# A graph kernel's attention weights: the second multiply of each group reads its exponentials in SBUF and not from a PSUM copy

## What is computed

```python
w_m = (efeat @ W_msg + b_msg).reshape(E, 16, 16)
w_a = (efeat @ W_attn + b_attn).reshape(E, 16, 16)
h_src = feat[src][:, :, None]
e1, e2 = w_m * h_src, w_a * h_src
ex = exp(e2 - segment_max(e2, dst)[dst])
attn = ex / segment_sum(ex, dst)[dst]
ft = segment_sum(e1 * attn, dst).sum(axis=1)
x = layernorm(x + ft)
x = layernorm(x + segment_mean(edge_attr, dst))
```

## Time and profile before

| what | us |
|---|---|
| median of 3 executions (2994.75 to 3017.14) | 3010.83 |
| span of the profiled execution, first to last instruction | 2950.2 |
| TensorE matmuls busy | 2137.9 (72%) |
| DVE (VectorE) busy | 1862.0 (63%) |
| POOL (GpSimd) busy | 1687.5 (57%) |
| ACT (ScalarE) busy | 1256.9 (43%) |
| mean granted TensorE clock | 0.861 |

### The profile page before, as it was taken

The page is one execution under the profiler, slowest core; times in us unless marked ns, Lnnn a source line. Parts: engine busy times, 40 slices in busy tenths (PEclk is TensorE's granted clock), DMA queues, the critical chain, the costliest instruction groups (busy, mean ns, idle before and its releaser), DMA issues. The chain is left out here.

```text
span 2950.2 us, 21765 instructions
## 1 busy us (share of the span) xinstructions
PE 2137.9 (72%) x6682; PEld 952.6 (32%) x6682; DVE 1862.0 (63%) x2907; ACT 1256.9 (43%) x1228; POOL 1687.5 (57%) x1845
## 2 busy tenths in 40 slices
PE   2347676676877777877787658877787767887777
PEld 1213233232333333333333223333333323333333
DVE  6246465566666666666676547766667656786776
ACT  3223443434444443454454325444444444554444
POOL 6556355665655565555565465655656565655633
PEclk8658888897988888989888889988989888988988
DMA  6000000000000000000000000000000001001000
GB/s 229 16 10 11 8 12 10 10 10 9 10 9 9 14 10 9 10 14 10 10 13 9 9 10 13 10 12 9 10 12 9 12 9 28 12 8 16 8 2 3
DMA packets 60073, 47.60 MB, mean 16 GB/s; under 512 B 28366, under 2 KB 55439, under 8 KB 59436
## 3 DMA queue, kind: packets, MB, share of 16 engines
q0 software_dynamic: 57632, 29.73, 8.0%
q1 hardware_dynamic: 2316, 16.38, 1.5%
HBM read 44.00 MB, written 1.90 MB: 16 GB/s over the span
## 5 line engine op out<-in xcount | busy, mean ns | idle before, releaser
L652 POOL DMA_INDIRECT AR<-in_xt,AR x1607 | 1538.8, 958 | 974.1 <-DVE AR L1472 491.3
L1128 PE MATMUL PX<-AR,CS 128*128 128x512 f32 x3246 | 1663.7, 642 | 37.8 <-issue 23.9
L1472 DVE CUSTOM_DVE_ANT_1 AR<-PW,AR 128x1024 f32<-128x1024 f32 x815 | 979.6, 1221 | 896.8 <-remote 651.2
L1108 PE MATMUL PW<-WS,LT 100*128 100x512 bf16 x1630 | 549.1, 423 | 683.9 <-DVE AR L1472 511.8
L1128 PEld LDWEIGHTS PX<-AR,CS 128*128 128x128 f32 x3246 | 664.9, 206 | 652.1 <-issue 532.4
L888 ACT ACTIVATE LT<-PTB 100x1024 bf16<-100x1024 bf16 (+1 forms) x221 | 211.2, 956 | 1005.7 <-remote 601.0
L1485 DVE TENSOR_TENSOR AR<-AR,PX 128x1024 f32<-128x1024 f32 (+1 forms) x442 | 501.0, 1134 | 121.3 <-ACT PX L944 76.0
L1108 PEld LDWEIGHTS PW<-WS,LT 100*128 100x128 bf16 x1630 | 141.5, 103 | 1113.7 <-DVE AR L1472 543.2
L946 ACT ACTIVATE AR<-AR 128x2048 f32<-128x2048 f32 (+1 forms) x221 | 412.9, 1869 | 7.2
L950 ACT ACTIVATE PX<-AR 128x1024 f32<-128x1024 f32 (+1 forms) x221 | 212.4, 961 | 412.3 <-DVE AR L1485 294.8
L944 ACT ACTIVATE PX<-AR 128x1024 f32<-128x1024 f32 (+1 forms) x221 | 231.0, 1045 | 39.4 <-DVE AR L1485 30.1
(11 more groups left out here) (192 smaller groups left out, 517.7 us busy)
## 6 DMA issues: line engine op xcount, KB each, us to landing
AR<-in_xt,AR POOLq DMA_INDIRECT x1607
AR<-in_eat SPq DMA_DIRECT2D x3, 3128.0 KB
AR<-in_eat SPq DMA_DIRECT2D x1, 3120.0 KB
y_d<-AR SPq DMA_DIRECT2D x1, 784.0 KB
AR<-y_d SPq DMA_DIRECT2D x1, 784.0 KB
AR<-in_es,E0I POOLq DMA_INDIRECT x48
y_d<-AR POOLq DMA_INDIRECT x36
CS<-in_cst SPq DMA_DIRECT2D x1, 442.0 KB, 5.3
```

Of the source, the lines that this page charges most:

```text
L652: g.indirect_dma_start(feat(h, j - j0, j - j0 + 1), None, xt, bass.IndirectOffsetOnAxis(ap=node, axis=0)).then_inc(hg_sem(h), 16)
L1108: i = pe.matmul(PAIRS[s % 2][:, j, :], LT[:, g % 3, lo:lo + 128], WS[:, :], start=True, stop=True)
L1128: i = pe.matmul(PDR, IDN, x, start=(a == 0 and j == 0), stop=(g == LAST[k] and j == n - 1))
L1472: v.tensor_tensor_reduce(em(g, j, j + 2).rearrange("p (x c) -> p x c", c=32), w, hb, 1.0, LOW, ALU.mult, ALU.max, accum_out=MXC[:, k % 2, ...
```

## The change

ScalarE's third pass (L950) and the two waits in front of it are gone, so ScalarE makes two passes. `gm(g, 1)` waits for the second pass (`a_exp`) and reads the exponentials where they lie, in `EMR`, beside the messages: its two inputs and its output are all in SBUF, in runs of 16 floats with a stride of 32. `gm(g, 0)` is as before. `EXP` is now free as soon as `gm(g, 0)` is done, so the next group's first pass waits for `v_gm` at 2c - 1 and not at 2c. The semaphore `a_x` counts once per group and not twice.

```diff
                         if c >= 1:
-                            a.wait_ge(S["v_gm"], 2 * c)
+                            a.wait_ge(S["v_gm"], 2 * c - 1)
                         a.activation(half(w), x[:, 0:w, :], ACT.Exp, bias=shift).then_inc(S["a_x"], 1)
-                        a.wait_ge(S["a_x"], 2 * c + 1)
+                        a.wait_ge(S["a_x"], c + 1)
                         a.activation(x, x, ACT.Exp, bias=shift).then_inc(S["a_exp"], 1)
-                    if c is not None:
-                        a.wait_ge(S["a_exp"], c + 1)
-                        a.wait_ge(S["v_gm"], 2 * c + 1)
-                        a.activation(half(w), x[:, w:2 * w, :], ACT.Copy).then_inc(S["a_x"], 1)
...
                 def gm(g, h):
                     w = 8 * GRP[g][2]
-                    v.wait_ge(S["a_x"], 2 * g + 1 + h)
-                    y = em(g).rearrange("p (x a o) -> p x a o", a=2, o=16)[:, w * h:w * h + w, 1, :]
-                    v.tensor_tensor(y, y, EXP[:, 0:16 * w].rearrange("p (x o) -> p x o", o=16), ALU.mult).then_inc(S["v_gm"], 1)
+                    y = em(g).rearrange("p (x a o) -> p x a o", a=2, o=16)[:, w * h:w * h + w, :, :]
+                    if h == 0:
+                        v.wait_ge(S["a_x"], g + 1)
+                        powers = EXP[:, 0:16 * w].rearrange("p (x o) -> p x o", o=16)
+                    else:
+                        v.wait_ge(S["a_exp"], g + 1)
+                        powers = y[:, :, 0, :]
+                    v.tensor_tensor(y[:, :, 1, :], y[:, :, 1, :], powers, ALU.mult).then_inc(S["v_gm"], 1)
```

## The result

| kernel | median, us | lowest to highest | profiled span | time of that execution |
|---|---|---|---|---|
| before | 3012.53 (4 executions) | 2994.75 to 3017.14 | 2950.2 | not recorded with its profile |
| after | 2929.38 (4 executions) | 2920.58 to 2939.08 | 2929.3 | 2931.18 |

The ratio is 0.9752, with a 95% interval of 0.9708 to 0.9797. The prediction was wrong, in its sign too.

A forecast was written before the change was run, and what follows sets the result against it. The prediction saw waits as the bound, with DVE held at its feature multiply until shortly after POOL's gather bursts pause. Its terms, -12 + 0 + 0 + 2 + 30 + 2 = +22 us on 3010.8, gave 3033 us, range 2985 to 3085.

The forecast's parts named there:

- the coupling: DVE's remote waits in front of L1472: a longer burst of POOL's gathers was said to hold DVE longer.
- the +30 us: What slower gathers on POOL cost in the end: +30 us, somewhat under half of bounds 0 and 71.
- the lengthening: POOL's gathers L652, held by multiplies with two SBUF inputs: mean from 958 to about 1,000 ns, 71 us in all.
- full price: Rival: every burst passes its lengthened gathers on to DVE, +63 us, 3074 us; chance 0.28.
- absorbed: Rival: POOL's longer gathers come wholly out of its own waits, -8 us, 3003 us; chance 0.14.
- relief: Rival: L888 and L944 are late because of L950, so other waits go too, -67 us, 2944 us; chance 0.12.
- the factor 0.77: Share of the time POOL is in a burst of gathers, applied to 92 us to give 71.
- The multiply: DVE's second multiply with two SBUF inputs instead of one: 1,226 against 1,217 ns, 2 us over 221.
- DVE held by POOL: DVE's multiplies slowed by gathers starting beside them: taken as 2 us, with 18 us as the bound.
- a rival at +60: Rival: a DVE multiply that finds a gather under way stands for its rest, 60 us more, 3093 us; chance 0.05.
- ScalarE's copy: Removing L950 lets DVE's second multiply start about 1.05 us earlier in 12 waits: -12 us.
- The 60.6 us: Difference between profiled span and timed median of the kernel before, taken as unchanged by the edit.

The follow-up runs named there:

- b1: The kernel before, unchanged, profiled again on a slower chip: 2984.48 us, ratio 1.0040.
- x10: The kernel before with one POOL memset of 128x1830 for each block, 48 of them: 2989.33 us, ratio 0.9926.
- x2_again: The changed kernel, but its second multiply reads the first half's exponentials in PSUM (wrong factors), on a slower chip: 2912.05 us, ratio 0.9909.
- x5_paced: The kernel before with an unused POOL memset of 128x360 behind each group's gathers: 2898.97 us, ratio 0.9858.
- x5_again: The kernel before with the POOL memset of 128x360 behind each group's gathers, run once more: 2958.93 us, ratio 0.9827.
- x1_again: The kernel before with its second multiply reading SBUF and ScalarE's copy kept, on a slower chip: 2885.42 us, ratio 0.9824.
- a0: The changed kernel itself, run again beside the kernel before on a slower chip: 2882.72 us, ratio 0.9787.
- x7: The changed kernel with a POOL memset of 128x360 behind each group's gathers: 2932.08 us, ratio 0.9761 to the kernel before.
- x8: The kernel before with a POOL memset of 128x1000 behind each group's gathers: 2866.91 us, ratio 0.9644.
- x4_again: The changed kernel with the first multiply reading SBUF too and one ScalarE pass, on a slower chip: 2805.53 us, ratio 0.9459 to before.
- x11: Both multiplies read SBUF, one ScalarE pass, plus a POOL memset of 128x500 behind each group's gathers: 2747.55 us, ratio 0.9218 to before.
- x9: Both multiplies read SBUF, one ScalarE pass, plus a POOL memset of 128x1000 behind each group's gathers: 2676.70 us, ratio 0.8949 to before.
- x12: The kernel before with a POOL memset of 128x900 twice in each group, inside its gathers: 2642.29 us, ratio 0.8834.
- x6: The kernel before with every second gather left out, so half the edges lack their features: 2197.74 us, ratio 0.7395.
- x1_port_only: The kernel before with its second multiply reading SBUF and ScalarE's copy kept, on the faster chip: 2335.13 us, ratio 1.0374.
- x4_both_sbuf: The changed kernel with the first multiply reading SBUF too and one ScalarE pass, on the faster chip: 2488.20 us, ratio 1.1049 to before.
- b0: The kernel before, unchanged, profiled on the faster chip: 2251.86 us, ratio 1.0003.
- x2_copy_only: The changed kernel, but its second multiply reads the first half's exponentials in PSUM (wrong factors), on the faster chip: 2248.41 us, ratio 0.9986.
- set 1: The first set of runs, all on one chip of the faster kind, where the kernel before takes 2251.8 us.

## Why the prediction was wrong

Side by side, from the profiles of the chips on which before takes 2943 us or more (the waits of POOL are those in front of the gathers and of L657 together). Each row of waits is one execution, and the rows come from three chips, so neighbours can't be told apart:

| kernel | POOL busy, us | POOL waits for DVE | DVE's remote waits | ratio |
|---|---|---|---|---|
| b1 (before) | 1688.5 | 660.5 | 681.4 | 1.0040 |
| x10, 48 pauses | 1765.2 | 612.1 | 720.8 | 0.9926 |
| x2_again, copy gone, gathers as before | 1686.3 | 586.3 | 619.8 | 0.9909 |
| x5_paced, 215 pauses | 1780.7 | 502.3 | 615.6 | 0.9858 |
| x5_again, 215 pauses | 1777.7 | 570.9 | 643.5 | 0.9827 |
| x1_again, lengthened gathers | 1768.0 | 506.5 | 596.6 | 0.9824 |
| a0 (after) | 1768.5 | 510.2 | 609.2 | 0.9787 |
| x7, after with 215 pauses | 1859.7 | 456.3 | 594.3 | 0.9761 |
| x8, 215 longer pauses | 1895.8 | 360.9 | 523.2 | 0.9644 |
| x4_again | 1885.6 | 315.6 | 526.5 | 0.9459 |
| x11 | 1990.8 | 173.5 | 432.7 | 0.9218 |
| x9 | 2088.0 | 34.8 | 159.2 | 0.8949 |
| x12, 412 pauses | 2047.2 | 53.0 | 288.2 | 0.8834 |
| x6, half the gathers | 942.8 | 889.5 | 32.8 | 0.7395 |

**The step that failed** is the coupling: "a burst that lasts longer holds DVE longer", and with it, under "What it does to POOL", the +30 us taken out of bounds of 0 and 71. The earlier trace rows show one stretch in which DVE goes on after POOL has paused, and I read from it that the hold lasts as long as the burst. The same trace had the counterexample. Of its 102 remote waits of DVE over 2 us in front of L1472, 58 end in a pause of POOL (over 0.6 us without an instruction) and 44 while its gathers run on, as here:

```profile
1747.96 0.94 POOL L652 DMA_INDIRECT AR<-in_xt,AR  x1 [0.30 <-issue]
1748.42 1.22 DVE L1472 CUSTOM_DVE_ANT_1 AR<-PW,AR 128x1024 f32<-128x1024 f32 x1 [8.59 <-remote]
1749.20 0.94 POOL L652 DMA_INDIRECT AR<-in_xt,AR  x1 [0.30 <-issue]
```

The table says what a slower POOL does in place of it: from b1 to x8 to x12 POOL's busy time rises by 207 and 359 us, with the same 1,607 gathers, and DVE's remote waits fall by 158 and 393 us. The runs fit a hold that hangs on how closely the gathers follow each other, and not on how long POOL's work between two waits lasts; that reading was not tested apart from the number and the place of the pauses, and x7, x10 and x4_again (526.5 us of remote waits beside x8's 523.2, at a lower ratio) don't lie on one line with the rest. Nor were the bounds wide enough: they held no gain, though nothing in the rows excluded one. I had written "I don't know the mechanism" and then let its sign be certain. Measured on its own, the lengthening was worth -52 us (x1_again; -39 to -64 by the interval) in place of +30. A lengthened gather comes out of POOL's waits for DVE (506.5 us are left, against 660.5 in b1 and 634.7 in before, on other chips or profiles), so it costs nothing, and it spreads the same gathers wider. That makes this case a fourth kind beside full price, absorbed and relief, which had no rival and no chance.

**The size of the lengthening was right.** Predicted: a mean of about 1,000 ns, 71 us in all, and an unchanged median. Measured: 998 ns, +64.3 us for L652 over the gathers of the earlier trace rows, and the busy time of all of POOL grew by 84.8 us (the block fetches L657 and the rest among it). In x1_port_only, where POOL never pauses, the prediction's estimate without the factor 0.77 is 73 + 19 = 92 us, and the measured growth 84.5: a little high in both. For x4_both_sbuf, with twice as many such multiplies, it would be 185 us, and 231.7 were measured, so the estimate doesn't carry that far. The mechanism, a gather held until the multiply has ended, stands.

**The full price is real, elsewhere.** +83.3 us for 84.5 us of gathers in x1_port_only, and 236.4 for 231.7 in x4_both_sbuf, is that rival to the letter, on the chip where POOL doesn't wait. My condition for it was turned round: I thought that the 651.2 us of held DVE speak for it and POOL's 635 us of waits against. The waits decide, and in every profile of before in which DVE is held POOL has these waits too. (By its own terms the rival needed 38 of the 71 us to cross 1%, and not 42: I left two terms of +2 out.)

**The multiply** lasts 1,221 against 1,217 ns; I had taken 1,226. Right. **DVE held by POOL** was taken as +2, with a rival at +60. That did not happen: in x1_port_only DVE's busy time is 1.7 us above that of b0, and of its second multiplies of 1,024 elements 101 start inside a running gather, of which none lasts longer than 1,230 ns. Right.

**ScalarE's copy** was taken as -12 us. By the rows that is what its wait was worth: DVE's 17.2 us for L950 became 4.1 us for L946. By the time it was too small where DVE is held (x2_again -27 us, interval -20 to -34) and too big where it is not (x2_copy_only -3.4 us). The rival of ScalarE's relief, at 2944 us, came nearest in its number, yet its reason is not borne out. In after TensorE's waits for L888 are 13.5 us lower (34.0 for 47.5) and DVE's for L944 21.4 us lower (54.6 for 76.0), but b1, with the copy, has 25.9 and 70.4, and a0, without it, 36.5 and 81.7. These waits vary as much between profiles as the rival wants to see. And x1_again gains its 52 us with the copy in place. Where the rest of the 27 us comes from is open.

**The 60.6 us** outside the span do not exist, as told above: the part outside is 1.9 us. The sum was made as a difference, so its sign did not hang on them.

**What stays open.** Why gathers hold DVE, and why on one chip they don't. In the trace of before DVE stands from 899.20 to 910.72, while the two products that it multiplies next ended at 897.90 and 900.05 by the timeline:

```profile
897.30 0.60 PE L1108 MATMUL PW<-WS,LT 100*128 100x512 bf16 x2
...
899.45 0.60 PE L1108 MATMUL PW<-WS,LT 100*128 100x512 bf16 x2
```

L1472 also waits until TensorE's sum has read the slots of `EMR` that it will overwrite. The trace's semaphore events show that increment late: the sum ends at 901.77, its increment stands at 910.61, 0.11 us before DVE goes on. Another late increment of TensorE's, of L1108, stands at 905.68, in the middle of the gathers. Over the whole trace of before, 389 of TensorE's 1,033 recorded increments come more than 1 us after the end of the last instruction that could have made them; of DVE's 1,358 that is so for 15, of ScalarE's 807 for 6. In b0 it is so for 3 of TensorE's, and in x6, with half the gathers, for 34 of 1,036. In x12 they are still 497 of 1,040, but those over 5 us late have become fewer, 110 in place of 170. So what holds DVE is that reports of finished work on TensorE come late where gathers are dense; why they do is not known. One rival was not tested: on the slower chips the recorded events themselves are incomplete (7,632 of the gathers' 24,752 landings in before, all of them in b0), so that whatever delays the increments may also touch the recording, or the recording may take part in it.

Which pattern of pauses is best is open too. Per us of pause, x10 gains 0.28 us, x5_paced 0.47, x5_again 0.58, x8 0.52 and x12 0.97, so shorter distances seem to be better, but the first three have wide intervals, and size, number and place of the pauses were not changed one by one.

## What to carry to other kernels

An engine that waited 635 us for another cost nothing when it was slowed by less than that, and brought a gain: ask of a coupling that you can't explain for both signs, and put the price from the other side into the bounds. The cheapest test of such a coupling is idle work on the engine that runs ahead, in the unchanged kernel. Time a change like this on more than one chip, and look at who waits for whom there first: the same edit was worth -1.8% or +3.7%, and POOL's waits in front of the gathers (491 us in before, 10 in b0) told the two kinds of chip apart.

## What was not expected of the hardware

- The same kernel takes 2251.8 us on one chip and 2943 to 3012 us on others, with 0 against 651 to 681 us of remote waits on DVE.
- With 815 gathers instead of 1,607, the slower kind of chip reaches 2197.7 us, with a mean granted TensorE clock of 0.957 against 0.862 in b1. On the chip of set 1 the kernel before has 0.956. So the lower mean clock of before (0.861) goes with its waits and is not a property of those chips.
- A gather that starts inside a DVE multiply with two SBUF inputs ends 0.82 us after it, in before and in after. The same multiply with one input in PSUM did that to none: in before, 228 gathers start inside an L1485 and 375 inside an L1472, and not one of them lasts over 1.0 us.
- On the slower chips TensorE's semaphore increments come late (in before 389 of 1,033 by more than 1 us, 45 of them by more than 10), and those of DVE and ScalarE hardly ever; with half the gathers nearly all of TensorE's are on time (34 of 1,036 late in x6).
